# One 128-row mask matmul in place of two 64-row ones in a decoder kernel

## The chip, the cores and the metric

The kernel runs on one core of a Trainium2 chip. The metric is device time in microseconds (us) of one execution. Before the change the median of three runs is 3727.97 us (3722.27 to 3732.47).

## The reference

Four decoder layers over x [4, 512, 128], post-normed, each with self-attention, cross-attention and a feed-forward or mixture-of-experts part. What the change touches is attention with 16 heads of 8 features, in which a triangle of the scores is masked before the softmax. Cut to that:

```python
# L0_xattn, first part, and L2_attn, first part: causal, 512 queries x 512 keys
w = einsum('bhqd,bhkd->bhqk', q, k) * scale
w = where(tril(ones(512, 512)), w, -inf)          # "causal"
# L2_attn, second part: 512 queries x 256 encoder keys, a bias per key
w = w + where(tril(ones(ql, kl), k=2) == 0, neg, 0) + extra_bias   # "tril2"
out = einsum('bhqk,bhkd->bhqd', softmax(w), v)
```

Each of the four batch units passes through L0s and L2s (causal) and L2c (tril2). A fourth masked attention, L1c, takes its mask over 77 keys as data ("given").

## The kernel before, in words

The whole model is one program. Attention is run by `segment(plan, weights)`, three times; the triangular masks lie in the first segment (L0s) and the second (L2s, L2c). A `Plan` makes one list, `order`, out of the jobs of the four units, by costs and due times written into it; every engine walks the same list and takes the items that are its own, in that order. The change does not touch `Plan`.

**Scores on TensorE.** Query and key features are split in three bf16 parts, so that one head's matmul contracts 51 rows (scores for the row maximum, "max" items, line 936, written to psM) or 53 rows (scores for the exponential, "exp" items, line 959, written to psE). Heads 0 to 7 lie on SBUF partitions 0 to 63 and heads 8 to 15 on 64 to 127 (`pair_and_half`): a head's matmul occupies one half of the array's rows, chosen by `lo`. A wide attention has four sets of four heads; sets 0 and 1 are in the lower half, 2 and 3 in the upper. The max items of a set stand in the order beside the exp items of the set before it. So for sets 0 and 2 of each attention the two kinds of item are in different halves, and for sets 1 and 3 in the same half.

**Masks on TensorE.** A mask of 0 and -2^100 (`masks_bf`, bf16) is added into the PSUM bank by a matmul with the identity (`ident_bf`) as weights, broadcast over the heads in the bank. `masked_heads` puts it in front of the heads where it covers their full width (the four-head banks of 128 keys, and some of tril2), and else behind them, on 128 or 256 columns of each head. The mask has 128 rows; `add_mask` (lines 864 to 874) issues two matmuls of 64 rows, both in the half in which the heads of that bank are. For this `ident_bf` and `masks_bf` hold a second copy with the halves swapped, made in the set-up by four DMAs (line 632). L1c alone uses `add_whole_mask` (line 880), one matmul over all 128 rows.

**Around them.** VectorE reduces two psM banks to row maxima (line 1243). ScalarE exponentiates one psE bank (line 1120). Each of the two is double-buffered: TensorE's max step n waits for reduction n-2, exp item n for the exponential n-2. TensorE further multiplies probabilities by values (line 979, 128 rows in four column strips of 32, f32), transposes (lines 716 and 1028, 128 rows) and projects (lines 989 to 1009), all with 128 rows, into psA and psB.

By the code a causal set has 11 masked banks for its max items and 11 for its exp items. The heads of either kind stream 5,120 columns; one pass of their masks streams 2,048. A tril2 set has 4 masked max banks (of 8) and 8 masked exp banks, 4,096 columns of heads and 1,536 of masks of either kind. There are 32 causal sets and 16 tril2 sets, so 32 x 22 + 16 x 12 = 896 masked banks.

Of the kernel before, what the change touches and what calls it, by code (L numbers as in the profile page):

```python
# [8 lines left out]
BF16 = mybir.dt.bfloat16  # L9
# [5 lines left out]
P = 128  # L15
# [492 lines left out]
def build(nc, io):  # L508
    ctx = ExitStack()
    with ctx:  # L510
# [19 lines left out]
        ident_bf = sb("ident_bf", [P, 2, P], BF16)  # L530
        masks_bf = sb("masks_bf", [P, 2, 6 * P], BF16)
# [65 lines left out]
        with Stage(nc, "cast", "zeroed", "halves_cast", "rolled", "row_parts", "own") as (  # L597
                block, cast, zeroed, halves_cast, rolled, row_parts, own):
# [8 lines left out]
            @block.sync  # L607
            def _(sp):
                sp.dma_start(row_f, io["rows"]).then_inc(loads, 16)
                sp.dma_start(mask_f, io["masks"]).then_inc(loads, 16)  # L610
                sp.dma_start(mask_q_i, io["mask_q"]).then_inc(loads, 16)
                sp.dma_start(mask_k_i, io["mask_k"]).then_inc(loads, 16)
                sp.dma_start(w_q8_i, io["w_q8"]).then_inc(loads, 16)
                sp.dma_start(e_b2[:], io["e_b2"]).then_inc(loads, 16)
                sp.dma_start(ctxT[:], io["ctxT"]).then_inc(loads, 16)
                sp.dma_start(pack[:], io["pack"]).then_inc(loads, 16)
                for b in range(B):
                    sp.dma_start(xt[:, b], io["x"].rearrange("b (t p) d -> p b t d", p=P)[:, b]).then_inc(loads, 16)
# [17 lines left out]
                sp.wait_ge(rolled, 16 * 6)  # L636
                sp.wait_ge(loads, 16 * 12)
# [19 lines left out]
            def _(dve):  # L657
# [4 lines left out]
                nc.vector.tensor_copy(ident_bf[:, 0, :], ident).then_inc(halves_cast, 1)  # L662
                nc.vector.tensor_copy(masks_bf[:, 0, :], mask_f).then_inc(halves_cast, 1)
# [90 lines left out]
        def segment(plan, weights):  # L754
# [65 lines left out]
            with Stage(nc, "max_scored", "max_taken", "exp_scored", "exp_taken", "pv_done", "x_full0", "x_full1",  # L820
# [39 lines left out]
                def _(pe):  # L860
# [16 lines left out]
                    def add_whole_mask(view, mask):  # L877

                        both, at, _, wide = mask
# [4 lines left out]
                    def masked_heads(out, n_heads, width, lo, mask, score):  # L884
# [3 lines left out]
                        if whole and lo is None:  # L888
                            add_whole_mask(view, mask)
                        elif whole:  # L890
                            add_mask(view, lo, mask, True)
# [3 lines left out]
                        if mask is not None and not whole:  # L895
                            last = add_mask(view[:, :, mask[2]:mask[2] + mask[3]], lo, mask, False)
                        return last

                    for item in order:
                        task, job = item[0:2]  # L900
                        if task == "max":
# [17 lines left out]
                            if not c.wide:  # L919
                                mask, base_bank = max_mask(c, t), 2 * (n % 2)  # L920
                                if mask is not None:
                                    for bank in range(2):
                                        add_whole_mask(psM[:, base_bank + bank, 0:HG * SC].rearrange(
                                            "p (h k) -> p h k", h=HG), mask)
# [11 lines left out]
                                out, len(heads), keys, lo, max_mask(c, t), lambda i, to, start, stop: nc.tensor.matmul(  # L936
# [5 lines left out]
                        elif task == "exp":  # L942
# [4 lines left out]
                            if i == 0:  # L947
# [10 lines left out]
                                out, len(heads), width, lo if c.wide else None, exp_mask(c, k),  # L958
# [1159 lines left out]
```

## Time and profile before

| | |
|---|---|
| median of 3 runs | 3727.97 us (3722.27 to 3732.47) |
| the profiled execution's own time | 3732.0 us |
| its span, first to last instruction | 3730.2 us |
| mean granted TensorE clock over the span | 0.805 of full |
| PE busy | 2921.4 us, 78% |
| VectorE busy | 1791.5 us, 48% |
| ScalarE busy | 1259.5 us, 34% |

A matmul is given in the rows as rows*weight columns, then what it streams: "64*128 64x512" contracts 64 rows, has 128 weight columns and streams 512 columns. The duration of one holds its way through the array as well as its streaming, so the distance between the starts of two matmuls, and not a duration, tells what one costs the engine. PE is the matmuls, PEld the weight loads.

### The profile page before, as it was taken

What the parts mean: (1) busy time and instruction counts of PE and PEld (TensorE: products, weight loads), DVE (VectorE), ACT (ScalarE), POOL (GpSimd) and SP (SyncE); (2) the same over time, 40 slices, a digit from 0 to 9 for tenths busy, and PEclk for the clock granted to TensorE, in tenths of its full rate; (3) what the DMA queues carried; (4) which work ended last, traced back from release to release, by engine and by line L of the source; (5) the groups of instructions that cost most, each with busy time, mean ns of one, the idle gap of its engine ahead of it and who ended that gap; (6) DMA issues with size and microseconds to landing.
All of it is one profiled execution on the core that took longest, in us unless ns stands there. A gap on an engine that the chain in (4) does not pass through costs nothing. (4 is left out here: it accounts for less than half of the span.)

```text
span 3730.2 us, 49027 instructions
## 1 busy us (share of the span) xinstructions
PE 2921.4 (78%) x18024; PEld 1500.0 (40%) x18024; DVE 1791.5 (48%) x3891; ACT 1259.5 (34%) x2170; POOL 534.5 (14%) x726
## 2 busy tenths in 40 slices
PE   2888888757887779977887777699999787357887
PEld 0222344332223236654443333376667222123665
DVE  3656554376655124445455333234443677233666
ACT  0456544412555231113445443311111321023332
POOL 3101111122111010011111111000000366400000
PEclk7678987855879679987789677699999888556998
DMA  3111111102110011213111000122222000100111
GB/s 94 24 26 22 27 27 22 20 1 35 18 24 17 11 32 63 68 32 44 23 23 27 17 11 11 38 83 86 63 68 63 1 1 0 27 15 29 61 59 46
DMA packets 89696, 126.58 MB, mean 34 GB/s; under 512 B 23142, under 2 KB 72358, under 8 KB 89203
## 3 DMA queue, kind: packets, MB, share of 16 engines
q1 hardware_dynamic: 88884, 121.03, 14.2%
q8 instruction: 146, 2.39, 0.3%
q10 hardware_dynamic: 576, 2.43, 0.2%
q14 instruction: 90, 0.74, 0.1%
HBM read 76.36 MB, written 1.05 MB: 21 GB/s over the span
## 5 line engine op out<-in xcount | busy, mean ns | idle before, releaser
L1243 DVE TENSOR_REDUCE maxima<-psM 128x2 f32<-128x1024 f32 (+4 forms) x640 | 682.6, 1082 | 796.7 <-PE psM L936 333.9
L1120 ACT ACTIVATE probs<-psE 128x512 f32<-128x512 f32 (+2 forms) x1248 | 709.0, 585 | 866.9 <-PE psE L959 507.6
L1604 PEld LDWEIGHTS psM<-values,probs 128*128 128x128 f32 x4096 | 491.9, 192 | 98.4 <-issue 96.9
L1604 PE MATMUL psM<-values,probs 128*128 128x128 f32 x4096 | 495.3, 276 | 0.0
L936 PE MATMUL psM<-k_stack,q_stack 51*128 51x512 bf16 (+3 forms) x1280 | 407.7, 392 | 68.4 <-DVE maxima L1243 31.7
L959 PE MATMUL psE<-q_stack,k_stack 53*128 53x512 bf16 (+3 forms) x1152 | 414.3, 399 | 32.7 <-ACT probs L1120 27.9
L1658 ACT ACTIVATE probs<-psM,pack 128x512 f32<-128x512 f32 x320 | 219.1, 687 | 637.2 <-PE psM L1596 637.2
L1672 DVE SCALAR_TENSOR_TENSOR hres<-psM,gates,hres 128x128 f32<-128x128 f32 x896 | 252.2, 344 | 337.6 <-PE psM L1604 336.7
L1596 PE MATMUL psM<-xT,values 128*128 128x512 f32 x640 | 343.6, 620 | 7.4 <-DMA values<-experts_dram 7.4
L936 PEld LDWEIGHTS psM<-k_stack,q_stack 51*128 51x128 bf16 x1280 | 107.3, 101 | 317.8 <-issue 212.3
L1687 DVE TENSOR_SCALAR probs<-psE,pack 128x512 f32<-128x512 f32 x192 | 142.8, 750 | 136.0 <-PE psE L1596 133.0
L979 PE MATMUL psA<-probs,values 128*32 128x256 f32 (+3 forms) x1856 | 198.8, 503 | 10.2 <-ACT probs L1120 4.7
L1596 PE MATMUL psE<-xT,values 128*128 128x512 f32 x384 | 200.8, 605 | 0.0
L1394 POOL TENSOR_SCALAR pool_t<-mean_var 128x4 f32<-128x4 f32 x60 | 14.8, 246 | 1198.3 <-DVE mean_var L1180 1192.1
L959 PEld LDWEIGHTS psE<-q_stack,k_stack 53*128 53x128 bf16 x1152 | 98.6, 97 | 213.0 <-ACT probs L1120 118.9
L871 PE MATMUL psM<-masks_bf,ident_bf 64*128 64x128 bf16 (+2 forms) x832 | 168.0, 288 | 2.5 <-DMA k_stack<-k_parts 2.4
L871 PE MATMUL psE<-masks_bf,ident_bf 64*128 64x128 bf16 (+2 forms) x960 | 168.3, 264 | 0.0
L979 PE MATMUL psB<-probs,values 128*32 128x256 f32 (+3 forms) x1472 | 152.9, 489 | 9.0 <-ACT o_raw L1137 3.3
L959 PE MATMUL psE<-q_stack,kc_stack 53*77 53x512 bf16 x256 | 113.0, 529 | 58.6 <-ACT probs L1120 25.4
L1939 POOL TENSOR_TENSOR yt<-yt 128x1024 f32<-128x1024 f32 x16 | 49.5, 3096 | 596.3 <-DVE yt L1918 596.3
L1596 PEld LDWEIGHTS psM<-xT,values 128*128 128x128 f32 x640 | 109.4, 200 | 57.0 <-issue 48.6
L1596 PEld LDWEIGHTS psE<-xT,values 128*128 128x128 f32 x384 | 75.7, 197 | 97.4 <-issue 94.3
(305 smaller groups left out, 3430.1 us busy)
## 6 DMA issues: line engine op xcount, KB each, us to landing
values<-experts_dram SPq DMA_DIRECT2D x128, 512.0 KB, 3.6
q_stack<-q_parts SPq DMA_DIRECT2D x432, 64.0 KB
k_stack<-k_parts SPq DMA_DIRECT2D x192, 64.0 KB
pack<-pack_dram SPq DMA_DIRECT2D x1, 4677.5 KB
kc_stack<-k_parts SPq DMA_DIRECT2D x192, 9.6 KB
q_stack<-max_rows SPq DMA_DIRECT2D x160, 4.0 KB
k_stack<-k_parts SPq DMA_DIRECT2D x48, 32.0 KB
k_stack<-in_w_dram ACTq DMA_DIRECT2D x1, 1536.0 KB, 6.4
```

Source lines behind the costliest of these rows:

```text
L871: last = nc.tensor.matmul(view, ident_bf[lo:lo + 64, side, 0:view.shape[0]], both[lo:lo + 64, side, at:at + wide].unsqueeze(1) .to_broadca ...
L936: out, len(heads), keys, lo, max_mask(c, t), lambda i, to, start, stop: nc.tensor.matmul(to, q_stack[lo:lo + R_MAX, job.a % Q_SLOTS, pair_ ...
L959: lambda h, to, start, stop: nc.tensor.matmul(to, ks[lo:lo + R_END, pairs[h], k * P:k * P + c.kn], q_stack[lo:lo + R_END, job.a % Q_SLOTS, ...
L979: last = nc.tensor.matmul(x_bank[b][32 * j:32 * j + 32, q0:q1], vs[:, k, 2 * pair + hb, :], probs[:, (e.key0 + k) % 2, j, q0:q1], start=k ...
L1120: nc.scalar.activation(probs[0:c.kn, m % 2, heads[0]:heads[-1] + 1, q0:S], psE[0:c.kn, n % 2, 0:len(heads) * (S - q0)].rearrange("p (h q) ...
L1243: nc.vector.tensor_reduce(top, psM[:, at:at + len(banks), 0:per * keys].rearrange("p b (h k) -> p b h k", h=per), AX_X, ALU.max, negate=Tr ...
L1596: nc.tensor.matmul(hidden_bank(n), w_of(j, True, f), xT[:, u, :], start=True, stop=True)\
L1604: last = nc.tensor.matmul(psO[:, j % 2, t * P:(t + 1) * P], probs[:, j % 2, f, t * P:(t + 1) * P], w_of(j, False, f), start=f == 0, stop=f ...
L1658: nc.scalar.activation(out, src, func, bias=bias).then_inc(act_h, 1)
L1672: last = nc.vector.scalar_tensor_tensor(out=hres[:, u, t, :], in0=psO[:, j % 2, t * P:(t + 1) * P], scalar=gates[:, u, t, e:e + 1], in1=hr ...
L1687: nc.vector.tensor_scalar(out, src, bias, 0.0, ALU.add, ALU.max).then_inc(dve_h, 1)
L1939: me.mark(nc.gpsimd.tensor_tensor(both, both, weighed[n % 2][:, :, 2:4, :], ALU.add))
```

## The change

`add_mask` issues one matmul that contracts all 128 rows, in place of two over 64 rows in the heads' half; `add_whole_mask` goes, `masked_heads` loses `lo`. The swapped second copies of `ident_bf` and `masks_bf` go, and with them the four DMAs of the set-up and the semaphore that held them back. Cut to its core:

```diff
-        ident_bf = sb("ident_bf", [P, 2, P], BF16)
-        masks_bf = sb("masks_bf", [P, 2, 6 * P], BF16)
+        ident_bf = sb("ident_bf", [P, 1, P], BF16)
+        masks_bf = sb("masks_bf", [P, 1, 6 * P], BF16)
...
-                sp.wait_ge(halves_cast, 2)
-                for both in (ident_bf, masks_bf):
-                    for lo in (0, 64):
-                        sp.dma_start(both[lo:lo + 64, 1, :], both[64 - lo:128 - lo, 0, :]).then_inc(rolled, 16)
...
-                    def add_mask(view, lo, mask, opens):
+                    def add_mask(view, mask, opens):
 
                         both, at, _, wide = mask
-                        for half_n in range(2):
-                            side = 0 if 64 * half_n == lo else 1
-                            last = nc.tensor.matmul(view, ident_bf[lo:lo + 64, side, 0:view.shape[0]],
-                                                    both[lo:lo + 64, side, at:at + wide].unsqueeze(1)
-                                                    .to_broadcast([64, view.shape[1], wide]),
-                                                    start=opens and half_n == 0, stop=not opens and half_n == 1)
-                        return last
...
+                        both = both if len(both.shape) == 2 else both[:, 0, :]
                         return nc.tensor.matmul(view, ident_bf[:, 0, 0:view.shape[0]],
                                                 both[:, at:at + wide].unsqueeze(1)
-                                                .to_broadcast([P, view.shape[1], wide]), start=True, stop=False)
+                                                .to_broadcast([P, view.shape[1], wide]), start=opens, stop=not opens)
```

The order of the engines' work stays as it was, but for the mask matmuls on TensorE and the four DMAs. Two places of TensorE's order follow; M is what writes psM, E what writes psE, and x2 at a row's end means two instructions alike. The first is in L0s, with M and E in different halves, from a transposition (L716) to the next values (L979). Before:

```order
L716 MATMUL psA<-pack,o_raw 128x128 x4
L936 MATMUL psM<-k_stack,q_stack 128x384
L871 MATMUL psM<-masks_bf,ident_bf 128x128 x2
L959 MATMUL psE<-q_stack,k_stack 128x384
L871 MATMUL psE<-masks_bf,ident_bf 128x128 x2
L936 MATMUL psM<-k_stack,q_stack 128x384
L871 MATMUL psM<-masks_bf,ident_bf 128x128 x2
L979 MATMUL psB<-probs,values 32x512 x4
L959 MATMUL psE<-q_stack,k_stack 128x384
```

After, with lines 712, 866, 920, 943 and 963 for 716, 871, 936, 959 and 979:

```order
L712 MATMUL psA<-pack,o_raw 128x128 x4
L920 MATMUL psM<-k_stack,q_stack 128x384
L866 MATMUL psM<-masks_bf,ident_bf 128x128
L943 MATMUL psE<-q_stack,k_stack 128x384
L866 MATMUL psE<-masks_bf,ident_bf 128x128
L920 MATMUL psM<-k_stack,q_stack 128x384
L866 MATMUL psM<-masks_bf,ident_bf 128x128
L963 MATMUL psB<-probs,values 32x512 x4
L943 MATMUL psE<-q_stack,k_stack 128x384
```

Each mask pair has become one matmul; nothing has moved. It now stands between matmuls of 51 or 53 rows with 128 rows of its own. The second place is a little earlier, with the four-head banks, whose masks of 512 columns stand in front of the heads. Before:

```order
L871 MATMUL psM<-masks_bf,ident_bf 128x128 x2
L871 MATMUL psE<-masks_bf,ident_bf 128x512 x2
L959 MATMUL psE<-q_stack,k_stack 128x128 x4
L871 MATMUL psM<-masks_bf,ident_bf 128x512 x2
L936 MATMUL psM<-k_stack,q_stack 128x128 x4
L979 MATMUL psA<-probs,values 32x256 x4
L959 MATMUL psE<-q_stack,k_stack 128x512
```

After:

```order
L866 MATMUL psM<-masks_bf,ident_bf 128x128
L866 MATMUL psE<-masks_bf,ident_bf 128x512
L943 MATMUL psE<-q_stack,k_stack 128x128 x4
L866 MATMUL psM<-masks_bf,ident_bf 128x512
L920 MATMUL psM<-k_stack,q_stack 128x128 x4
L963 MATMUL psA<-probs,values 32x256 x4
L943 MATMUL psE<-q_stack,k_stack 128x512
```

Here too the pairs have become single matmuls and the rest stands as it was.

## Rows read from the trace of the kernel before

**Rows 1.** The page, part 2: busy tenths of PE and its granted clock in 40 slices of 93 us.

```profile
PE   2888888757887779977887777699999787357887
...
PEclk7678987855879679987789677699999888556998
```

**Rows 2.** Windows: PE, PEld, DVE, ACT, POOL busy us (instructions); granted clock; DMA share; GB/s.

```profile
374.00:672.00 298.00, 252.22 (x2284) 124.70 (x2283) 149.38 (x245) 138.39 (x265) 44.68 (x76) 0.83 0.15 24
1694.00:2238.00 544.00, 436.73 (x3401) 216.29 (x3402) 246.65 (x423) 253.77 (x438) 72.34 (x132) 0.80 0.13 23
```

**Rows 3.** The page, part 5: the mask matmuls of line 871, psM and psE.

```profile
L871 PE MATMUL psM<-masks_bf,ident_bf 64*128 64x128 bf16 (+2 forms) x832 | 168.0, 288 | 2.5 <-DMA k_stack<-k_parts 2.4
L871 PE MATMUL psE<-masks_bf,ident_bf 64*128 64x128 bf16 (+2 forms) x960 | 168.3, 264 | 0.0
```

**Rows 4.** Waits from 374 to 672 us: who waited for the masked score banks.

```profile
DVE maxima L1243 <- PE psM L871: 127.9, 64, 6.1
ACT probs L1120 <- PE psE L871: 127.1, 109, 4.2
```

**Rows 5.** Timeline of PE, 463.0 to 463.95 us: start us, us, engine, line, op.

```profile
462.81 0.49 PE L716 MATMUL psA<-pack,o_raw 128*128 128x128 f32 x3
463.24 0.33 PE L936 MATMUL psM<-k_stack,q_stack 51*128 51x384 bf16 x1
463.25 0.33 PE L959 MATMUL psE<-q_stack,k_stack 53*128 53x384 bf16 x1
463.41 0.22 PE L871 MATMUL psM<-masks_bf,ident_bf 64*128 64x128 bf16 x1
463.42 0.22 PE L871 MATMUL psE<-masks_bf,ident_bf 64*128 64x128 bf16 x1
463.47 0.21 PE L871 MATMUL psM<-masks_bf,ident_bf 64*128 64x128 bf16 x1
463.48 0.21 PE L871 MATMUL psE<-masks_bf,ident_bf 64*128 64x128 bf16 x1
463.52 0.32 PE L936 MATMUL psM<-k_stack,q_stack 51*128 51x384 bf16 x1
463.69 0.27 PE L871 MATMUL psM<-masks_bf,ident_bf 64*128 64x128 bf16 x2
463.89 0.64 PE L979 MATMUL psB<-probs,values 128*32 128x512 f32 x4
```

**Rows 6.** The same timeline asked from 463.2 us on: the last L716 alone.

```profile
463.03 0.27 PE L716 MATMUL psA<-pack,o_raw 128*128 128x128 f32 x1
```

**Rows 7.** Timeline of PE about 563 us, at half clock.

```profile
562.95 0.31 PE L871 MATMUL psM<-masks_bf,ident_bf 64*128 64x128 bf16 x1
563.19 1.08 PE L979 MATMUL psA<-probs,values 128*32 128x512 f32 x4
```

**Rows 8.** Timeline of PE about 438 us: the four-head banks, both in one half.

```profile
438.12 0.39 PE L959 MATMUL psE<-q_stack,k_stack 53*128 53x128 bf16 x4
438.35 0.59 PE L871 MATMUL psM<-masks_bf,ident_bf 64*128 64x512 bf16 x2
438.78 0.39 PE L936 MATMUL psM<-k_stack,q_stack 51*128 51x128 bf16 x4
439.09 0.42 PE L979 MATMUL psA<-probs,values 128*32 128x256 f32 x4
```

**Rows 9.** Timeline of PE about 1253 us: L1c, its 128-row mask beside 53-row heads.

```profile
1252.46 0.41 PE L880 MATMUL psE<-ctx_mask_k,ident_bf 128*77 128x512 bf16 x1
1252.80 0.41 PE L959 MATMUL psE<-q_stack,kc_stack 53*77 53x512 bf16 x1
```

**Rows 10.** Waits of PE from 374 to 672 us, the longest.

```profile
PE psB L716 <- ACT o_raw L1137: 6.6, 7, 1.6
```

**Rows 11.** Timeline of the set-up: the queue's (SPq) last mask copies and VectorE's last memset.

```profile
30.17 1.24 SPq L632 DMA_DIRECT2D masks_bf<-masks_bf  x2
...
35.58 3.47 DVE L678 MEMSET probs<- 128x4096 f32 x1 [1.03 <-issue]
```

More of the change, by code:

```diff
@@ L595, in build @@
         loads3 = ctx.enter_context(nc.semaphore("loads3"))
-        with Stage(nc, "cast", "zeroed", "halves_cast", "rolled", "row_parts", "own") as (
-                block, cast, zeroed, halves_cast, rolled, row_parts, own):
+        with Stage(nc, "cast", "zeroed", "rolled", "row_parts", "own") as (
+                block, cast, zeroed, rolled, row_parts, own):
             mask_q_i = work[:, 0, 0:QT * SC].bitcast(I32)
@@ L635, in _ @@
                 sp.dma_start(rows[2:3, :], row_low).then_inc(rolled, 16)
-                sp.wait_ge(rolled, 16 * 6)
+                sp.wait_ge(rolled, 16 * 2)
                 sp.wait_ge(loads, 16 * 12)
@@ L661, in _ @@
                 dve.wait_ge(loads, 16 * 12)
-                nc.vector.tensor_copy(ident_bf[:, 0, :], ident).then_inc(halves_cast, 1)
-                nc.vector.tensor_copy(masks_bf[:, 0, :], mask_f).then_inc(halves_cast, 1)
+                nc.vector.tensor_copy(ident_bf[:, 0, :], ident)
+                nc.vector.tensor_copy(masks_bf[:, 0, :], mask_f)
                 nc.vector.tensor_scalar(ctx_mask_q[:], mask_q_i, 0.0, MASKED, ALU.is_equal, ALU.mult)
@@ L864, in bank_x, with masked_heads @@
                         return x_bank[b], x_full[b]
-                    def add_mask(view, lo, mask, opens):
+                    def add_mask(view, mask, opens):
                         both, at, _, wide = mask
-                        for half_n in range(2):
-                            side = 0 if 64 * half_n == lo else 1
-                            last = nc.tensor.matmul(view, ident_bf[lo:lo + 64, side, 0:view.shape[0]],
-                                                    both[lo:lo + 64, side, at:at + wide].unsqueeze(1)
-                                                    .to_broadcast([64, view.shape[1], wide]),
-                                                    start=opens and half_n == 0, stop=not opens and half_n == 1)
-                        return last
-                    def add_whole_mask(view, mask):
-                        both, at, _, wide = mask
+                        both = both if len(both.shape) == 2 else both[:, 0, :]
                         return nc.tensor.matmul(view, ident_bf[:, 0, 0:view.shape[0]],
                                                 both[:, at:at + wide].unsqueeze(1)
-                                                .to_broadcast([P, view.shape[1], wide]), start=True, stop=False)
-                    def masked_heads(out, n_heads, width, lo, mask, score):
+                                                .to_broadcast([P, view.shape[1], wide]), start=opens, stop=not opens)
+                    def masked_heads(out, n_heads, width, mask, score):
                         view = out[:, 0:n_heads * width].rearrange("p (h k) -> p h k", h=n_heads)
                         whole = mask is not None and mask[3] == width
[L888 to L891, printed above, removed]
+                        if whole:
+                            add_mask(view, mask, True)
                         for i in range(n_heads):
@@ L895, in masked_heads @@
                         if mask is not None and not whole:
-                            last = add_mask(view[:, :, mask[2]:mask[2] + mask[3]], lo, mask, False)
+                            last = add_mask(view[:, :, mask[2]:mask[2] + mask[3]], mask, False)
                         return last
@@ L922, in _ @@
                                     for bank in range(2):
-                                        add_whole_mask(psM[:, base_bank + bank, 0:HG * SC].rearrange(
-                                            "p (h k) -> p h k", h=HG), mask)
+                                        add_mask(psM[:, base_bank + bank, 0:HG * SC].rearrange(
+                                            "p (h k) -> p h k", h=HG), mask, True)
                                 for i in range(HG):
@@ L935, in _ @@
                             last = masked_heads(
-                                out, len(heads), keys, lo, max_mask(c, t), lambda i, to, start, stop: nc.tensor.matmul(
+                                out, len(heads), keys, max_mask(c, t), lambda i, to, start, stop: nc.tensor.matmul(
                                     to, q_stack[lo:lo + R_MAX, job.a % Q_SLOTS, pair_of(base + heads[i][1]),
@@ L957, in _ @@
                             last = masked_heads(
-                                out, len(heads), width, lo if c.wide else None, exp_mask(c, k),
+                                out, len(heads), width, exp_mask(c, k),
                                 lambda h, to, start, stop: nc.tensor.matmul(
```

## The prediction

> **What bounds the kernel now.** I read the slices first, then the windows of the two stretches with triangular masks, then the waits there, then single matmuls in the timeline. The slices show where TensorE works and at what clock; it is granted either 2.4 GHz ("full") or 1.2 GHz ("half"), and a digit is the mean of both [rows 1]. The masks lie from 374 to 672 us and from 1694 to 2238 us. In these 842 us PE is busy 252.2 + 436.7 = 689 us, so it stands idle 153 us; VectorE and ScalarE are busy about half the time [rows 2]. The waits say who is late: VectorE waits 127.9 us and ScalarE 127.1 us in the first stretch for banks whose last matmul is a mask [rows 4]; PE's longest wait sums to 6.6 us [rows 10]. TensorE sets the pace of both stretches. What the change does to TensorE there is what it does to the time, less what PE's idle time takes up.
>
> **What one matmul costs.** The distance of starts is the price. At full clock 384 columns take 0.16 us and 128 take 0.053 to 0.06 (463.52, then 463.69; 463.41, then 463.47) [rows 5]. Three things are to be seen in those rows.
>
> First, halves run side by side. Head M starts at 463.24 and head E at 463.25; each half then does its masks, also 0.01 us apart. In the order, M's masks stand ahead of head E, and E's head starts before them all the same. The engine overtakes between halves.
>
> Second, a change between matmuls over half of the array's rows and over all of them costs time in which nothing streams. The two masks begun at 463.69 have streamed by 463.80, and L979 (128 rows) starts at 463.89: 0.09 us [rows 5]. The other way round: from 462.81 to 463.03 are two L716, so one takes 0.11 [rows 5, 6]; the last starts at 463.03 and the 51-row head at 463.24, 0.10 us more. L1c shows the very pair that the change makes, a 128-row mask and then a 53-row head: 0.34 us for 512 columns, which stream in 0.213, so 0.127 with 77 weight columns [rows 9]. At half clock, a mask of 128 columns (0.107 us) and then L979: 0.24 us, so 0.135 [rows 7]. Within one half nothing of the kind shows: two 512-column masks and then a head come 0.43 us after the first mask's start (438.35 and 438.78), the bare columns [rows 8].
>
> Third, since both halves have to be empty for a 128-row matmul, it ends the overlap too.
>
> **The change, part by part.**
>
> *Columns.* 1792 mask matmuls [rows 3] become 896. By the counts of a set: a causal set has 5,120 + 2 x 2,048 = 9,216 columns now for M and as many for E. Sets 0 and 2 run M and E beside each other, so the engine needs 9,216; sets 1 and 3 need 18,432. After it, with no overlap left, each needs 2 x 5,120 + 2 x 2,048 = 14,336. Over 32 sets: 16 x 9,216 + 16 x 18,432 = 442,368 now and 458,752 after. For the 16 tril2 sets (4,096 and 1,536): 172,032 now and 180,224 after. The sum grows by 24,576 columns. The granted clock is 0.83 and 0.80 there [rows 2], so about 0.81 x 2.4 = 1.94 columns per ns: **+13 us**. Half as many matmuls, and no stream saved: what the single mask saves where M and E share a half is what the lost overlap costs where they don't.
>
> *Changes of height.* I counted them along TensorE's order, masks as one and as two. In the first segment there are 1156 now and 1620 after, in the second 474 and 1106: 1096 more. (896 masks could add 1792; many stand beside values or transpositions, which have 128 rows anyway, and two masks of neighbouring banks may meet.) A clock of 0.81 is full for 0.62 of the time. I take 0.095 us at full clock, between the two ways, and 0.135 at half: 0.62 x 0.095 + 0.38 x 0.135 = 0.110 us each, **+121 us**. The bounds are 0.09 for all (+99) and 0.135 for all (+148).
>
> *The two places shown.* First place, from the head M at 463.24 to L979 at 463.89: 0.65 us now. After: three heads of 0.16, three masks of 0.053, five changes of 0.095 (the last mask goes over into L979 without one) make 1.11 us, so +0.46. Second place, from the E mask at 437.69 (the order gives it; its head comes at 438.12) to L979 at 439.09: 1.40 us now; after, two masks of 0.213, eight heads of 0.055 and four changes make 1.25, so -0.15. Only masks of 512 columns gain, 96 of the 896; most masks have 128 columns.
>
> *Idle time takes some up.* Gross it is 13 + 121 = 134 us. PE idles 153 us in the stretches [rows 2], much of it before a transposition that waits for a copy by ScalarE (seven times, 0.9 us each) [rows 10]. That copy stands behind ScalarE's exponentials, which wait for TensorE, so the wait moves along rather than shrinks; where matmuls lie between the values and the transposition it shrinks. In the first banks of a segment, where M runs alone, VectorE may hide some. Bounds: nothing, or half (-67). I take a fifth: **-27 us**.
>
> *The clock.* It may be granted at another share once the stretches run differently. Slices 5 to 7, with causal masks, have 9, 8, 7 tenths and PE at 8; slices 9 and 10 have 5 and 5 with PE at 5 and 7, slices 23 to 26 have 6, 7, 7, 6 with PE at 7, 7, 7, 6 [rows 1] (other work, but with more gaps). A fall from 0.81 to about 0.76 lengthens some 400 us of streaming by 25 us, of which I take **+15 us**; bounds 0 and +45.
>
> *Set-up.* Four DMAs and the wait for two casts go from the queue. The last of them was issued by 31.4 us, and VectorE's last memset runs to 39.05 us and ends the stage [rows 11]: 0. Without that cover the gain would be the 2.5 us of four issues. A smaller tile in SBUF costs and brings nothing.
>
> Sum: 134 - 27 + 15 = +122 us. The profiled execution took 3732.0 us, 4 above the median; against the median 3728 the forecast is **3850 us**.
>
> The Trainium skill, page "TensorE: Matmul & The Clock Gate" (Part 3, what overlaps), says that matmuls start and end in strict program order, only weight loads being pulled ahead. The rows show the contrary for starts in different halves [rows 5]. By that rule there would be little overlap to lose, the columns would count as 180,224 fewer (-93 us), and the sum would be 121 - 93 = +28 us.
>
> **The rivals.**
>
> *A, little overlap is lost.* M and E go on beside each other in spite of the masks between them, or most of their overlap comes where no mask stands. Then the columns give -90,112 (only shared halves save) to -46 us in place of +13, and the changes of height still cost 99 to 121: +40 to +75 gross, 3760 to 3795. For it: the engine overtakes. Against: a 128-row mask needs both halves.
>
> *B, the engine switches for free: faster.* The identity's weights are the same for every mask. If their load across all rows ran ahead beneath the heads, a change of height to or from a mask would cost nothing; with the overlap kept, 90,112 columns at 1.94 per ns go, -46 us, of which idle time (other engines become late next) gives back some 11: 3693 us. It decides from a price per change under about 0.04 us. Against it is L1c, where 128-row identity masks pay 0.127 us into a head [rows 9]. The same page of the Trainium skill (Part 2, on LDWEIGHTS) has loads pulled ahead when row groups don't conflict or when they go to the background buffer, which by itself would speak for this rival.
>
> *C, the waits swallow it.* PE's idle 153 us exceed the 134 us. If nearly all of it were slack, the time would be 3728 to 3739. Against: the waits of VectorE and ScalarE for masks are 20 times PE's longest [rows 4, 10].
>
> *D, the clock falls and nothing is absorbed.* 148 + 13 + 45 = +206 us or somewhat more: 3935.
>
> **How the numbers follow.** Forecast 0.66, A 0.15, D 0.11, B 0.04, C 0.04. A measurement of this kernel can tell about 0.3% (11 us) from no change. C gives "same", B gives "faster", the rest "slower": 0.04, 0.04, 0.92. The range leaves out B, C, and the outer parts of A and D: 3785 to 3935, and takes in half of the idle time absorbed (134 - 67 = +67, 3795) and the high price of a change with the clock's bound (+206).
>
> **What would show it.** Right: 896 mask matmuls of 128 rows; about 0.15 us from the start of a 128-column mask to that of the head behind it at full clock; head M and head E no longer 0.01 us apart where a mask stands between them; VectorE and ScalarE waiting longer for mask matmuls in both stretches; the stretches some 40 and 80 us longer, all others as they were. Wrong: heads of two halves still side by side across a mask (A), masks followed by heads after 0.06 us (B), PE's idle time shrunk by over 100 us (C), or clocks under 0.75 in the stretches (D).

## The result, and the profile after

| | before | after |
|---|---|---|
| median of 4 runs | 3725.12 us (3720.5 to 3732.47) | 3996.81 us (3992.76 to 4012.35) |
| ratio | | 1.0735 (1.0701 to 1.077) |
| the profiled execution's own time | 3732.0 us | 4012.35 us |
| mean granted clock over the span | 0.805 | 0.752 |

The change costs 272 us. The forecast was 3850 us with a range up to 3935: the sign is right, the size is less than half of what came. Here and below a ratio and its interval are worked out over the fast runs alone, so it can differ a little from the quotient of two medians. The page of the changed kernel, its head and its slices (now of 100 us each):

```profile
span 4010.6 us, 47231 instructions
...
PE   2888999875887779979999977779999987527887
...
PEclk7689655665687879985555776769999988656898
```

Where the masks are (slices 5 to 8 and 19 to 25), PE has more nines and the clock more fives and sixes than in [rows 1]. The windows, from the first triangular mask to the last of either stretch (columns as in [rows 2]), of the changed kernel:

```profile
365.50:776.30 410.80, 389.14 (x1926) 135.14 (x1925) 149.96 (x245) 141.14 (x264) 44.67 (x76) 0.62 0.11 17
1807.20:2517.40 710.20, 639.41 (x2853) 223.37 (x2853) 244.23 (x423) 257.97 (x438) 71.64 (x131) 0.61 0.10 17
```

And of the kernel before, cut in the same way:

```profile
374.60:671.70 297.10, 251.32 (x2279) 124.42 (x2276) 149.38 (x245) 138.15 (x264) 44.68 (x76) 0.83 0.15 24
1694.70:2238.00 543.30, 436.73 (x3401) 216.29 (x3402) 246.65 (x423) 253.77 (x438) 71.74 (x131) 0.80 0.13 23
```

So they grew by 114 and 167 us, 281 in all, and each of the three other parts of the program kept its length to within some 9 us. PE is busy 1028.6 us in place of 688, its idle time there falls from 152 to 92 us, and the granted clock from 0.83 and 0.80 to 0.62 and 0.61. VectorE and ScalarE do the same work in the same busy time, and wait longer for masked banks than in [rows 4]:

```profile
DVE maxima L1227 <- PE psM L866: 233.4, 78, 6.6
ACT probs L1104 <- PE psE L866: 228.4, 146, 4.5
```

PE's own longest wait is down from 6.6 us to 3.9. The mask matmuls of the page, in place of [rows 3], are 896 with 128 rows:

```profile
L866 PE MATMUL psE<-masks_bf,ident_bf 128*128 128x128 bf16 (+2 forms) x480 | 149.2, 312 | 0.0
L866 PE MATMUL psM<-masks_bf,ident_bf 128*128 128x128 bf16 (+2 forms) x416 | 139.0, 335 | 2.3 <-DMA k_stack<-k_parts 2.3
```

Now the two places that were shown. The second one, with the four-head banks, in the timeline of PE at full clock:

```profile
440.77 0.39 PE L920 MATMUL psM<-k_stack,q_stack 51*128 51x512 bf16 x1
441.09 0.23 PE L866 MATMUL psM<-masks_bf,ident_bf 128*128 128x128 bf16 x1
441.16 0.38 PE L866 MATMUL psE<-masks_bf,ident_bf 128*128 128x512 bf16 x1
441.47 0.40 PE L943 MATMUL psE<-q_stack,k_stack 53*128 53x128 bf16 x4
441.79 0.39 PE L866 MATMUL psM<-masks_bf,ident_bf 128*128 128x512 bf16 x1
442.12 0.40 PE L920 MATMUL psM<-k_stack,q_stack 51*128 51x128 bf16 x4
442.44 0.64 PE L963 MATMUL psA<-probs,values 128*32 128x256 f32 x8
```

From the E mask at 441.16 to L963 at 442.44 it is 1.28 us; 1.25 was predicted, 1.40 was the time before. A head of 512 columns streams in 0.213 us and its mask starts after 0.32: 0.107 us in which nothing streams. A 512-column mask and the head behind it are 0.31 and 0.33 us apart: 0.10 to 0.12. Two masks in a row (441.09, 441.16) are 0.07 us apart, 0.01 more than the first one streams: between them nothing is paid.

The first place, which ran at half clock in this execution:

```profile
474.89 0.50 PE L920 MATMUL psM<-k_stack,q_stack 51*128 51x384 bf16 x1
475.32 0.29 PE L866 MATMUL psM<-masks_bf,ident_bf 128*128 128x128 bf16 x1
475.54 0.50 PE L943 MATMUL psE<-q_stack,k_stack 53*128 53x384 bf16 x1
475.98 0.29 PE L866 MATMUL psE<-masks_bf,ident_bf 128*128 128x128 bf16 x1
476.20 0.50 PE L920 MATMUL psM<-k_stack,q_stack 51*128 51x384 bf16 x1
476.63 0.29 PE L866 MATMUL psM<-masks_bf,ident_bf 128*128 128x128 bf16 x1
476.85 1.08 PE L963 MATMUL psB<-probs,values 128*32 128x512 f32 x4
```

In [rows 5] heads M and E began 0.01 us apart; here M, mask, E, mask, M, mask follow one another, 1.96 us in place of 0.65. Of these 1.96 us the three heads and three masks at half clock are 1.28 us of streaming, and six changes of height at 0.11 to 0.12 (0.43 less 0.32; 0.22 less 0.107) are 0.68. There are six and not five: the last mask, 128 rows too, pays 0.11 us into the column strips of L963. So the place tripled because three things met: the heads no longer overlap, the changes, and a clock at half.

### The profile page after: what moved, and what is told of

It reads as the page before. It is cut to its first block and busy times, and to the rows that moved or that the text cites. A ratio compares the mean times of both kernels' runs of the same rounds, so it can differ in the third digit from the quotient of the medians.

```text
span 4010.6 us, 47231 instructions
## 1 busy us (share of the span) xinstructions
PE 3257.9 (81%) x17128; PEld 1517.6 (38%) x17128; DVE 1790.3 (45%) x3891; ACT 1266.8 (32%) x2170; POOL 535.3 (13%) x726
## 5 line engine op out<-in xcount | busy, mean ns | idle before, releaser
L920 PE MATMUL psM<-k_stack,q_stack 51*128 51x512 bf16 (+3 forms) x1280 | 457.7, 430 | 62.2 <-DMA k_stack<-k_parts 31.2
L943 PE MATMUL psE<-q_stack,k_stack 53*128 53x512 bf16 (+3 forms) x1152 | 463.5, 444 | 20.1 <-ACT probs L1104 18.6
L963 PE MATMUL psA<-probs,values 128*32 128x256 f32 (+3 forms) x1856 | 226.7, 568 | 6.0 <-ACT o_raw L1121 3.1
L963 PE MATMUL psB<-probs,values 128*32 128x256 f32 (+3 forms) x1472 | 173.0, 548 | 4.9 <-ACT o_raw L1121 3.3
L866 PE MATMUL psE<-masks_bf,ident_bf 128*128 128x128 bf16 (+2 forms) x480 | 149.2, 312 | 0.0
L866 PE MATMUL psM<-masks_bf,ident_bf 128*128 128x128 bf16 (+2 forms) x416 | 139.0, 335 | 2.3 <-DMA k_stack<-k_parts 2.3
```

The source lines that it names most:

```text
L920: out, len(heads), keys, max_mask(c, t), lambda i, to, start, stop: nc.tensor.matmul(to, q_stack[lo:lo + R_MAX, job.a % Q_SLOTS, pair_of(b ...
L943: lambda h, to, start, stop: nc.tensor.matmul(to, ks[lo:lo + R_END, pairs[h], k * P:k * P + c.kn], q_stack[lo:lo + R_END, job.a % Q_SLOTS, ...
L963: last = nc.tensor.matmul(x_bank[b][32 * j:32 * j + 32, q0:q1], vs[:, k, 2 * pair + hb, :], probs[:, (e.key0 + k) % 2, j, q0:q1], start=k ...
```

## Where 281 us came from

I added up, over every matmul of the two stretches, the columns that it streams by the clock of its moment, counting what two halves streamed at once a single time. Before this is 573 us, after it is 771. Before, both halves stream at once for 51 + 83 = 134 us; after, for 8 + 27 = 35. Matmuls of half height next to ones of full height (in the order in which they started, the few matmuls of three rows left aside) are 684 before and 1777 after.

- Columns: at full clock the 573 us would be 456 and the 771 would be 458. So as good as nothing was added: **+3**.
- Clock: while TensorE streamed it was granted 0.796 before (456.0 of 572.9) and 0.594 after (458.1 of 770.8). The 458.1 us at 0.796 would be 576, so the lower clock is 771 - 576 = **+195**.
- Changes: 1093 more at 0.11 us are +120; some 112 places where a mask now changes into column strips add 12: **+132**.
- Idle time of PE: **-60**.

The sum is 270 us, of the 281 measured. Some 6 us of the rest, by an estimate, are the 400 or so changes of before that stand beside values and transpositions and cost 0.04 us more at half clock than at full ([rows 5, 7]). That is bookkeeping; what lowers the clock it can't say. The experiments are about that.

## The experiments

Times are medians, and each ratio is against runs of the kernel before made beside them on the same chip; times from different groups of runs differ by up to 27 us for the same kernel (the kernel before: 3702 to 3729). Five kernels leave out all of the triangular masking (e1_nomask), or the half or all of it by masks of zeros (e2_one64, e10_same_one64; e3_thin64, e4_thin128). They compute something else and serve for their time alone.

**Is it the masks' work at all?** Three kernels ask what the pairs cost the kernel before.

e1_nomask: the two functions that hand out the masks hand out none for the triangular attentions.

```diff
-            if c.masks == "causal":
-                return masks_bf, 0, t * P, P
-            if c.masks == "tril2" and t < 2:
-                return masks_bf, 2 * P, t * P, (2 - t) * P
```

> The kernel before without its triangular masks (the given mask of L1c stays): the work of masking is left out. It is the floor from which both ways of masking are measured. Now the masks stream 360,448 columns, partly in one half while the other half streams heads. Both theories: some 3600 to 3640 us, so that the masks of the kernel before cost 90 to 130 us and those of the change 360 to 400 us. The granted clock in the two stretches tells the theories apart later: as high as in the kernel before (0.80 to 0.83) if what lowers it is what the 128-row masks bring.

Measured: 3674.73 us against 3718.99, ratio 0.9886 (0.9762 to 1.001). Expected were 3600 to 3640 with a clock of 0.80 or more in the stretches; in windows of about the two stretches it is 0.71 and 0.72:

```profile
355.00:651.00 296.00, 238.10 (x1530) 83.54 (x1526) 148.41 (x243) 135.82 (x263) 44.75 (x76) 0.71 0.15 24
1650.00:2190.00 540.00, 397.75 (x2392) 156.09 (x2396) 256.45 (x455) 257.41 (x449) 79.29 (x151) 0.72 0.15 25
```

e2_one64: a single matmul over 64 rows per bank.

```diff
-                        for half_n in range(2):
...
+                        return nc.tensor.matmul(view, ident_bf[lo:lo + 64, 0, 0:view.shape[0]],
+                                                both[lo:lo + 64, 0, at:at + wide].unsqueeze(1)
+                                                .to_broadcast([64, view.shape[1], wide]),
+                                                start=opens, stop=not opens)
```

> The kernel before with one 64-row mask matmul per bank in the heads' half in place of two, filled with zeros, so half of the mask is left out and the other half has no effect. It issues as many mask matmuls and mask columns as the change, but never changes height and never ends the overlap of the halves. Theory 1 (the changes of height and the lost overlap, and a clock that falls in their train, make the whole loss): between the kernel without masks and the kernel before, about 3670 us, clock 0.80 or more in the stretches. Rival 2 (the loss lies in something else that came with single masks): clearly above 3725 us.

Measured: 3694.0 us, ratio 0.994 (0.9899 to 0.9981), 24 us above the expectation.

e3_thin64: pairs as before, but each on 8 columns of a head.

```diff
+                        view, wide = view[:, :, 0:8], 8
                         for half_n in range(2):
```

> The kernel before with its pairs of 64-row mask matmuls cut to 8 columns a head and filled with zeros, all behind the heads: the masking is left out, the instructions stay. It prices 1792 short matmuls without a change of height. Both theories: 10 to 50 us above the kernel without masks, clock as there.

Measured: 3706.59 us, ratio 0.9964 (0.9911 to 1.0016), as expected some 30 us above the kernel without masks.

In the kernel before the triangular masks are worth about 1%, all of them together, and by the interval of e1_nomask perhaps nothing. The windows of e2_one64, with half of the mask columns gone:

```profile
356.10:651.00 294.90, 246.18 (x1928) 102.96 (x1925) 147.55 (x244) 137.27 (x264) 44.78 (x76) 0.76 0.15 24
1662.20:2205.60 543.40, 424.50 (x2857) 182.07 (x2858) 247.19 (x423) 252.28 (x438) 71.80 (x131) 0.74 0.13 23
```

Both stretches are as long as before (294.9 and 297.1; 543.4 and 543.3); the clock is lower (0.76 and 0.74) and PE little less busy. Less mask work came back as a lower clock, here and without any masks. So the change had almost nothing to win, even where its single mask saves a stream; and that TensorE sets the pace of both stretches, as the prediction has it, doesn't mean that work taken from it is time won.

e4_thin128: the changed kernel with its masks on 8 columns of a head, all of them behind the heads (those of the four-head banks stood in front), which makes some 60 changes of height more.

```diff
+                        if len(both.shape) == 3:
+                            both, view, wide = both[:, 0, :], view[:, :, 0:8], 8
```

> The change with its 128-row mask matmuls cut to 8 columns a head and filled with zeros, all behind the heads: the masking is left out, all changes of height and the lost overlap stay, the 180,224 mask columns go. Theory 1 (gaps and lost overlap are what the granted clock follows): the clock stays low, about 0.6 in both stretches, and the time is 3870 to 3930 us. Rival 2 (it is the streaming of mask columns through all 128 rows that keeps the clock low): the clock comes back to about 0.8 and the time is about 3765 us: some 3620 for the floor, 1200 changes at 0.10 make 120, lost overlap of the heads makes 55, less 30 of waits.

Measured: 3959.97 us, ratio 1.0653 (1.0523 to 1.0783); the change itself is 1.0735. Its windows:

```profile
369.30:757.70 388.40, 364.68 (x1927) 139.01 (x1925) 147.25 (x245) 141.51 (x265) 44.72 (x76) 0.58 0.12 18
1764.80:2470.10 705.30, 632.25 (x2849) 240.44 (x2848) 245.22 (x423) 258.89 (x438) 71.12 (x131) 0.54 0.10 17
```

Nearly all of the loss is still there, and so is the low clock; the time is 30 us above what the first theory expected. So most of the loss doesn't need the mask's columns, but only that a 128-row matmul stands there.

**Is it the second mask matmul, or the standing there?** e5_twice128: each triangular mask is issued twice over 128 rows. Two masks in a row pay no further change of height.

```diff
+                        for n in range(passes):
+                            last = nc.tensor.matmul(view, ident_bf[:, 0, 0:view.shape[0]],
...
+                                                    start=opens and n == 0, stop=not opens and n == passes - 1)
```

> The change with every triangular mask added twice by 128-row matmuls: 896 matmuls and 180,224 columns more, no further change of height and no further loss of overlap. At the clock of the changed kernel's stretches (0.62 of full, 1.49 columns per ns) the columns are 121 us. Theory 1 (the granted clock follows how much TensorE streams between gaps, so that added streaming pays for itself in clock): the clock rises to 0.66 to 0.72 in the stretches and the time grows by 10 to 60 us only, 4005 to 4055. Rival 2 (changes of height hold the clock down whatever streams): clock 0.62 as before and 90 to 120 us more, about 4100.

Measured: 4099.8 us (4084.49 to 4115.1), ratio 1.1074 (1.089 to 1.1258).

```profile
367.10:829.30 462.20, 444.71 (x2277) 147.90 (x2277) 147.64 (x245) 142.75 (x264) 44.74 (x76) 0.60 0.10 16
1844.20:2592.00 747.80, 680.23 (x3396) 236.61 (x3397) 245.23 (x423) 260.10 (x438) 71.83 (x131) 0.66 0.10 16
```

180,224 more columns cost 89 us by the two stretches (1210 us in place of 1121), 103 us by the medians and some 125 us by the ratios: 0.5 to 0.7 ns each, where full clock would be 0.42 and half 0.83. In the changed kernel TensorE is what these stretches wait for, and what is added to it is paid. By its time this is the outcome of the expectation's second rival; by the clock it lies between the two, 0.60 in the first stretch and 0.66 in the second. In the kernel before twice as many mask columns were nearly free (e1_nomask).

**The overlap by itself.** e6_same_half keeps the pairs of 64 rows, so it has none of the changes of height, and takes the overlap away: the second and third sets of four heads change places. The planner starts the max items of a set when the exponentials of the set two before it begin, so what stands beside each other is now always in one half.

```diff
+SET_AT = (0, 2, 1, 3)
...
-        return (HG * g + j) % 8, (HG * g + j) // 8
+        return (HG * SET_AT[g] + j) % 8, (HG * SET_AT[g] + j) // 8
```

> The kernel before with the second and third set of heads of each wide attention exchanged, so that score items for the maximum and for the exponential that stand side by side in the order are in the same half of the array, where they were in opposite halves: the overlap of halves goes, with no change of height and no column more. The trace of the kernel before shows 134 us of streaming that lies beneath other streaming in the two masked stretches, and more in the unmasked wide attentions. Theory 1 (lost overlap alone costs only part): 3760 to 3850 us, the clock in the stretches 0.85 or more, since the engine streams more of the time. Rival 3 (lost overlap is the main cost of the change): 3900 us or more.

Measured: 4352.34 us, ratio 1.1756 (1.1689 to 1.1824), clock over the span 0.68. The exchange takes in all wide attentions, those without a triangular mask too. Its windows:

```profile
486.10:926.70 440.60, 416.75 (x2280) 195.59 (x2277) 150.14 (x245) 142.20 (x265) 44.66 (x76) 0.54 0.11 16
2072.50:2859.40 786.90, 714.95 (x3400) 341.05 (x3402) 244.52 (x423) 259.25 (x438) 71.79 (x132) 0.54 0.09 16
```

Same matmuls, same sizes, same order, other halves: the two stretches take 1227.5 us in place of 840.4. And PE is busy for 92% of them (1131.7 of 1227.5), against 82% before, and is granted 0.54 against 0.81. The timeline of PE shows the one-after-the-other at half clock:

```profile
471.01 0.60 PE L939 MATMUL psM<-k_stack,q_stack 51*128 51x512 bf16 x1
471.41 0.63 PE L962 MATMUL psE<-q_stack,k_stack 53*128 53x512 bf16 x1
471.84 0.63 PE L939 MATMUL psM<-k_stack,q_stack 51*128 51x512 bf16 x1
472.26 0.63 PE L962 MATMUL psE<-q_stack,k_stack 53*128 53x512 bf16 x1
```

0.43 us for each 512 columns, and none beside it. This is what the third rival of the expectation described (the overlap is the main cost, 3900 us or more), and Theory 1 (3760 to 3850, clock 0.85 or more) did not.

e7_same_half128 is the changed kernel with the same exchange, so the change on a ground where there is no overlap to lose.

> The change with the same exchange of head sets. Its 128-row masks have ended nearly all overlap in the masked stretches already (35 us of 134 is left by its trace); the unmasked wide attentions lose theirs. Theory 1: above the changed kernel by less than the exchange costs the kernel before, 4010 to 4060 us, and hardly longer in the masked stretches themselves. If the masks had left the overlap alone, the exchange would cost as much here as there.

Measured: 4337.68 us, ratio 1.1717 (1.1616 to 1.1818).

```profile
498.30:947.40 449.10, 430.22 (x1926) 141.55 (x1925) 147.09 (x245) 142.29 (x264) 44.78 (x76) 0.55 0.10 16
2078.50:2844.80 766.30, 695.02 (x2852) 237.40 (x2853) 246.48 (x423) 259.23 (x438) 71.67 (x131) 0.58 0.10 16
```

Expected were 4010 to 4060 us; the exchange costs far more outside the masked stretches than was thought (some 250 us here and some 265 in e6_same_half). Within the two stretches it adds 387 us to the kernel before (840 to 1227) and only 94 to the changed one (1121 to 1215): there most of the overlap had gone already. Against e6_same_half the change costs nothing, 4352 to 4338 us. e10_same_one64 takes that nothing apart: the exchange, with one matmul of 64 rows per bank, so the columns of the change without its changes of height.

> The kernel with exchanged head sets (no overlap of halves) and one 64-row mask matmul of zeros per bank in place of two: half of the mask is left out. Against the exchange on the change (4338 us) it has the same columns and matmuls and 1,094 changes of height fewer (and about 110 fewer between masks and values), with no overlap to lose in either. Where changes of height cost 0.11 us each it takes 4200 to 4240 us; if they cost nothing where nothing overlaps, about 4338. Against the exchange on the kernel before (4352 us) it has 180,224 columns fewer, 139 us at the clock of 0.54: both readings must agree.

Measured: 4195.13 us, ratio 1.1276 (1.117 to 1.1381), at the lower end of what was expected if changes cost 0.11 us each.

```profile
495.00:888.00 393.00, 365.74 (x1928) 152.67 (x1925) 147.34 (x244) 141.49 (x264) 44.62 (x76) 0.55 0.12 18
2017.40:2710.40 693.00, 611.85 (x2855) 264.86 (x2856) 244.69 (x423) 257.90 (x438) 71.37 (x131) 0.56 0.10 18
```

Half as many mask columns save 4352 - 4195 = 157 us, where 139 were expected; going from 64 to 128 rows costs 4338 - 4195 = 143 us, some 0.12 us for each of about 1,200 changes. (The kernel before took 3702 us beside the one and 3729 beside the other; by the ratios, on 3702 us, it is 178 and 163 us, 0.14 for a change.) On this ground the two cancel. On the real one half as many mask columns save only 25 us (e2_one64), so the first gain is missing, and the lost overlap goes on top.

**Giving the overlap back.** e8_grouped128 keeps the 128-row masks and moves 257 of them: where two neighbouring banks are both masked behind their heads, TensorE does heads, heads, mask, mask. Cut to its core, with `hold` true for the first bank of such a pair:

```diff
                         if mask is not None and not whole:
-                            last = add_mask(view[:, :, mask[2]:mask[2] + mask[3]], mask, False)
+                            held.append([view[:, :, mask[2]:mask[2] + mask[3]], mask, None])
+                            if not hold[0]:
+                                last = add_held()
```

> The change with the order of 257 pairs of neighbouring masked banks altered: heads of both, then masks of both, in place of heads, mask, heads, mask. All matmuls and columns are the same; each pair makes two changes of height fewer (514 of 1778) and its heads may overlap again. Theory 1: 514 x 0.11 = 57 us less, overlap of some 100,000 columns back (about 60 us), and a higher clock (0.66 to 0.72): 3830 to 3900 us. If the number of changes and the overlap did not matter and the loss were in the 128-row masks as such, it would stay at 3997.

Measured: 3751.26 us (3748.72 to 3753.81), ratio 1.0133 (1.0079 to 1.0186), well under the 3830 to 3900 expected. The same kernel again, e11_grouped128_again:

> The grouped form of the change again, with more rounds: 1.010 to 1.018 of the kernel before. With the form that keeps 64-row pairs at 1.00 the difference is what some 580 changes of height cost where the overlap is mostly kept: gross 64 us, measured 40 to 60.

3756.74 us, ratio 1.01 (1.004 to 1.0161), the lower end of what was expected. And the change again beside it, e12_change_again:

> The change itself on the same chip, so that it stands beside the others: 1.07 to 1.077 of the kernel before.

3991.93 us, ratio 1.0722 (1.0641 to 1.0802). The grouping gives back 3991.93 - 3756.74 = 235 us, of the 263 that the change costs there. Windows and a piece of the timeline of e8_grouped128:

```profile
369.30:688.40 319.10, 285.46 (x1926) 106.93 (x1925) 148.53 (x245) 140.32 (x264) 44.72 (x76) 0.77 0.14 22
1691.80:2253.40 561.60, 468.95 (x2853) 182.31 (x2853) 246.71 (x423) 256.81 (x438) 71.74 (x131) 0.78 0.13 22
```

```profile
477.38 0.33 PE L956 MATMUL psM<-k_stack,q_stack 51*128 51x384 bf16 x1
477.38 0.39 PE L981 MATMUL psE<-q_stack,k_stack 53*128 53x512 bf16 x1
477.70 0.23 PE L866 MATMUL psM<-masks_bf,ident_bf 128*128 128x128 bf16 x1
477.77 0.22 PE L866 MATMUL psE<-masks_bf,ident_bf 128*128 128x128 bf16 x1
```

Both heads begin at 477.38 and the masks come together behind them: no mask parts the two heads. Both halves stream at once for 33 + 55 = 88 us again, the clock is back at 0.77 and 0.78, and the changes of height are 1263 in place of 1777. Those 514 fewer at 0.11 us are 57 us; the other some 180 us are overlap and clock.

e9_grouped64 is the check on the order: the kernel before, pairs of 64 rows, grouped in the same way.

> The kernel before, its 64-row mask pairs kept, with the order of the same 257 pairs of banks altered as in the grouped form of the change: heads of both, then masks of both. No change of height is added. Since the engine overtakes between halves, this order should make no difference: 3700 to 3735 us, the same as the kernel before. Then what the grouped 128-row form takes more is the price of its changes of height, and not of its order. If the order itself brought something, it would be faster than before.

Measured: 3723.22 us, ratio 0.9958 (0.9903 to 1.0012). The order alone is worth nothing. So e8_grouped128 gained because its 128-row masks stopped parting the heads, and by its fewer changes of height. What still parts it from e9_grouped64 (1.0133 and 1.01 against 0.9958, about 1.6% or 60 us) is about the price of its 579 changes more than before, 64 us.

**More overlap than before.** e13_more_overlap is the kernel before with 90 triples of TensorE's order turned from max, values, exp to max, exp, values; the max and the exp are then neighbours, in different halves.

```diff
+                    for n1, n2, n3 in zip(mine, mine[1:], mine[2:]):
+                        if [order[n][0] for n in (n1, n2, n3)] == ["max", "values", "exp"] and order[n3][2] > 0:
+                            pe_order[n2], pe_order[n3] = order[n3], order[n2]
```

> The kernel before with TensorE's order altered at some hundred places: where a score item for the maximum, a group of value matmuls and a score item for the exponential follow each other, the last two are exchanged, so that the score items of opposite halves meet and two changes of height less are made. If overlap is worth what the exchange of head sets says, each meeting saves 0.2 to 0.3 us at most, some 10 to 30 us in all: 3695 to 3715, less what later value matmuls delay on ScalarE. If overlap gained in small doses is taken up by waits: no difference that can be told, 3725.

Measured: 3676.74 us (3654.43 to 3693.07, 6 runs) against 3720.8, ratio 0.9875 (0.9833 to 0.9916): a little faster than the kernel before, beyond the scatter, and more than the 3695 to 3715 expected. Its windows:

```profile
371.30:667.30 296.00, 245.33 (x2280) 122.40 (x2277) 148.05 (x245) 136.62 (x265) 44.69 (x76) 0.81 0.15 24
1687.60:2212.80 525.20, 415.21 (x3401) 205.40 (x3402) 246.38 (x423) 251.26 (x438) 71.81 (x132) 0.81 0.14 23
```

Both halves stream at once for 58 + 89 us (51 + 83 before), and the changes of height are 620 in place of 684, which at 0.10 us is 6 us; this kernel doesn't tell the two apart. The second stretch is 18 us shorter. The first keeps its length but for 1 us: PE is busy for 6 us less there and idle for 5 more. 14 us more came behind the second stretch (1478.5 us in place of 1492.2); what they are I haven't looked into, and single runs of this kernel differ by more than that.

## Why the prediction was right and wrong

**The step that failed is "The clock".** It put +15 us, with 45 as its bound; by the bookkeeping above it is +195. All of the miss is in it, since the other terms were off by +11 (changes), -10 (columns) and -33 (idle time), -32 together. Both of its factors were too small: it took some 400 us of streaming where 573 stream, and a fall from 0.81 to 0.76 where the clock of the stretches fell to 0.61. The reasoning was that the clock is low where PE has gaps, and the slices with gaps were read for its size. e6_same_half refutes that: fewer gaps, 92% busy, and a clock of 0.54. With the overlap taken away the clock of the masked stretches went from 0.83 and 0.80 to 0.54, and where e8_grouped128 gave the overlap back it was 0.77 and 0.78. The forecast removed the overlap in one term and all but kept the clock in the next.

**The changes of height**, +121 predicted, about +132. 1093 more in the trace against 1096 counted. The price was taken as 0.095 at full clock and 0.135 at half, which holds for changes beside values and transpositions (medians 0.09 to 0.10 and 0.13 to 0.14 in either trace). The new ones, between masks and heads, cost 0.10 to 0.11 at full and 0.11 to 0.12 at half, so about 0.11 all the same. "The last mask goes over into L979 without one" was wrong: it pays 0.11 us. Into a transposition (L712, also 128 columns) a mask goes without, within 0.03 us.

**The columns**, +13 predicted, +3 came. That it is so near is in part luck, for two errors work against each other. The prediction let M and E share a half in sets 1 and 3. In fact the max items of a set stand beside the exp items two sets before, so of neighbouring max and exp banks in the order 1200 are in opposite halves and 29 in one. The description of the kernel has this wrong too. On the other hand neighbours overlap only part of the time. By the prediction 204,800 columns of overlap were to go, 106 us at 1.94 per ns; 134 - 35 = 99 us went, the 35 at a lower clock.

**The idle time** took up 60 us where 27 were predicted, within the bound of 67.

**The two places.** The second: 1.28 us against 1.25 predicted. The first: 1.11 predicted at full clock; in the trace it runs at half, 1.96.

**What was to be seen if right** was seen: 896 mask matmuls; masks and heads one behind the other; 0.17 us from mask to head (435.86 to 436.03 below, 0.15 predicted); longer waits of VectorE and ScalarE; all other stretches as they were. Only the stretches grew by 114 and 167 us, not by 40 and 80.

```profile
435.86 0.23 PE L866 MATMUL psM<-masks_bf,ident_bf 128*128 128x128 bf16 x1
436.03 0.33 PE L943 MATMUL psE<-q_stack,k_stack 53*128 53x384 bf16 x1
```

**The rivals.** A and B fall by these rows, C by the idle time, which shrank by 60 us and not by over 100. D named the right mechanism and its sign, clocks under 0.75, and priced it at the bound of 45 us that the slices seemed to give. The bound was wrong, not only the choice within it. It had been read from a few slices, where nothing said what the clock followed. And the prediction calls them places with other work, but slices 23 and 24 (2051 to 2238 us) lie in the second masked stretch, at 0.68 and 0.71: the kernel before had a low clock beside masks already.

By the rule of strict program order of starts (the Trainium skill, "TensorE: Matmul & The Clock Gate", Part 3) the sum would have been +28 us. The runs speak against it again: in one program order the halves start together [rows 5], and e9_grouped64, which writes that order out, changes nothing measurable. The Trainium skill, "TensorEngine Tiling (Array Packing)", Key Properties, says that changing the tiling mode drains TensorE, and names no price. The trace agrees, with 0.10 to 0.12 us for each change between masks and heads.

## What to carry to other kernels

Where matmuls use half of the array's rows, look in the timeline for two that start together before putting a matmul of all rows between them. Here it cost 0.11 us on each side, and above that it parted what ran side by side. Two passes in the half that is being used can be free where one pass over everything isn't; and if it must be the whole array, put such matmuls together (heads, heads, mask, mask), which gave back 235 of 263 us here. When a change alters what runs side by side, don't carry the granted clock over from the trace before. And before taking work from a busy TensorE, try what leaving it out altogether gives: here it was 1% of the time, the rest came back as a lower clock.

## What the runs showed of the hardware

- The granted clock of a busy TensorE. With one half streaming at a time it was 0.54 at 92% busy (e6_same_half), with both halves often together 0.83 and 0.80 at 82%. What it follows isn't settled. It isn't the time of overlap alone: the changed kernel has 35 us of it and 0.62 and 0.61, e6_same_half also about 35 (13 + 21) and 0.54. It isn't the number of changes of height: with no overlap left it is about the same with few of them (e6_same_half, 0.54) and with many (e7_same_half128, 0.55 and 0.58). With less mask work it fell while the time hardly moved (e2_one64 0.76 and 0.74, e1_nomask 0.71 and 0.72). The runs change overlap and clock together, so how much of the 195 us a kernel with the overlap lost and the clock kept would have paid stays open.
- The price of a change of height between a bf16 mask and a head hardly depends on the clock: 0.10 to 0.11 us at full, 0.11 to 0.12 at half. Between f32 values or transpositions and heads or 64-row masks it does: 0.09 to 0.10 at full, 0.13 to 0.14 at half. A price is paid as well between a mask and values, of 128 rows both, whose columns are strips of 32 (0.11).
- Starts overtake between the halves of the array (463.25 before 463.41 in [rows 5], against the order); no row shown has it within a half.
